# A state-space layer and a mixture of experts in one launch: the moments of z1 taken by squares on ACT, the projection put between the two shared down products, and the first tile table made from six groups

## The reference

```python
def reference(x, A, B, C, D, gamma, beta, router_weight, ...):   # x: 2 x 2048 x 256, float32
    xB = einsum('bsd,nd->bsn', x, B)
    state = tanh(state @ A.T + xB_t)              # a scan over the 2048 steps
    y = einsum('bsn,dn->bsd', states, C) + D * x + x
    x = layernorm(x + layernorm(y) * gamma + beta)          # x2
    # router: sigmoid, the better of 2 groups of 4 experts, the best 2 of its 4, weights divided by their sum
    routed = sum over the 2 chosen e of w_e * (silu(x @ w_gate[e]) * (x @ w_up[e])) @ w_down[e]
    shared = (silu(x @ sw_gate) * (x @ sw_up)) @ sw_down
    return layernorm(x + routed + shared)
```

## Time and profile before

| | |
|---|---|
| median of three runs | 330.69 us (330.62 to 330.85) |
| the profiled execution, its own time | 330.8 us |
| its span, first to last instruction | 329.1 us |
| scan, first pass, and loads | to about 44 us |
| seven periods | about 44 to 161 us; from p = 2 on one is 14.72 us |
| group 7 and first table | to 176.5 us |
| 43 tiles | 176.5 to about 315 us |
| busy, share of the span | PE 83%, DVE 70%, POOL 50%, ACT 47% |

### The profile page before, as it was taken

The page is one execution under the profiler, slowest core; times in us unless marked ns, Lnnn a source line. Parts: engine busy times, 40 slices in busy tenths (PEclk is TensorE's granted clock), DMA queues, the critical chain, the costliest instruction groups (busy, mean ns, idle before and its releaser), DMA issues.

```text
span 329.1 us, 7496 instructions
## 1 busy us (share of the span) xinstructions
PE 274.0 (83%) x2237; PEld 225.2 (68%) x2237; DVE 229.9 (70%) x912; ACT 154.9 (47%) x354; POOL 163.4 (50%) x302
## 2 busy tenths in 40 slices
PE   4998997788888989886476899999999999999920
PEld 4897986687777878775354567777777777677610
DVE  4366977769898989889893688866666656656630
ACT  1464522554445465453520445655655655654620
POOL 3102004037686776768643426545555555555571
PEclk9999999799999999999676699999999999999995
DMA  5898920001130303022136823545444353431100
GB/s 178 273 279 260 375 96 2 0 2 67 67 122 11 133 0 132 33 101 89 43 132 189 253 84 72 156 124 154 116 133 135 89 143 121 121 95 51 34 7 0
DMA packets 21002, 36.79 MB, mean 112 GB/s; under 512 B 3029, under 2 KB 9694, under 8 KB 20961
## 3 DMA queue, kind: packets, MB, share of 16 engines
q1 hardware_dynamic: 16336, 23.50, 24.9%
q0 software_dynamic: 4624, 12.79, 10.2%
HBM read 20.00 MB, written 17.71 MB: 115 GB/s over the span
## 4 chain that ended last, share of the span: by engine, by line
PE 65%; DVE 11%; SPq 6%; issue 6%; ACT 5%; POOL 3%; DMA 2%; POOLq 1%; DVEq 0%
PE bank L658 21%; PE bank L685 11%; PE bank L602 5%; PE bank L614 4%; PE bank L549 4%; PE bank L546 4%; PE bank L506 4%; SPq L410 4%; PE bank L626 3%; PE bank L673 3%; PE bank L513 2%; PE bank L561 2%; DMA rows<-in_L_attn_x_dram 2%; DVE st L992 2%; ACT xT L805 2%
## 5 line engine op out<-in xcount | busy, mean ns | idle before, releaser
L658 PE MATMUL bank<-w,xTt 128*128 x516 | 69.7, 280 | 7.9 <-ACT xTt L823 2.2
L658 PEld LDWEIGHTS bank<-w,xTt 128*128 128x128 f16 x516 | 45.4, 99 | 36.4 <-issue 30.3
L1429 POOL DMA_INDIRECT out_dram<-xT,where x43 | 44.6, 1037 | 36.1 <-ACT xT L841 28.8
L1195 DVE SCALAR_TENSOR_TENSOR th_<-bank,tw,tsg 128x128 f32<-128x128 f32 x86 | 26.2, 346 | 34.1 <-ACT tsg L829 32.5
L829 ACT ACTIVATE tsg<-bank,g_un 128x256 f32<-128x256 f32 x43 | 20.4, 474 | 60.4 <-PE bank L658 60.4
L685 PE MATMUL bank<-wd,thT 128*128 x172 | 46.6, 393 | 0.1
L1415 POOL DMA_INDIRECT xs_dram<-rows,slot_i x32 | 33.5, 1046 | 18.1 <-issue 10.7
L506 PE MATMUL bank<-xT,BT 128*128 128x128 f32 x256 | 41.0, 284 | 0.0
L1372 POOL TENSOR_TENSOR rstd<-mv,eps 128x2 f32<-128x2 f32 (+2 forms) x38 | 10.4, 275 | 53.3 <-DVE mv L1209 21.9
L506 PEld LDWEIGHTS bank<-xT,BT 128*128 128x128 f32 x256 | 35.0, 196 | 0.4
L1376 POOL TENSOR_TENSOR rstd<-rstd,neghalf 128x2 f32<-128x2 f32 (+2 forms) x38 | 32.2, 848 | 0.6
(11 more groups left out here) (188 smaller groups left out, 540.1 us busy)
## 6 DMA issues: line engine op xcount, KB each, us to landing
xT<-xs_dram SPq DMA_DIRECT2D x43, 262.0 KB, 3.0
rows<-in_L_attn_x_dram SPq DMA_DIRECT2D x7, 512.0 KB, 7.1
xs_dram<-cmp SPq DMA_DIRECT2D x1, 3144.0 KB, 14.5
wd<-in_L_ffn_w_down_dram SPq DMA_DIRECT2D x1, 1024.0 KB, 10.2
out_dram<-xT,where POOLq DMA_INDIRECT x43, 2.7
rows<-in_L_attn_x_dram SPq DMA_DIRECT2D x2, 256.0 KB, 3.6
xs_dram<-rows,slot_i POOLq DMA_INDIRECT x32, 3.0
xs_dram<-cmp SPq DMA_DIRECT2D x1, 262.0 KB, 15.8
```

What stands on the lines that cost most here:

```text
L658: last = pe.matmul(ps_tu(j)[:, r, :, :].rearrange("p w i -> p (w i)"), xTt[:, j % 2, 2 * px + k, :], w16[:, pw, bass.ds(e, 1), k, :, :].re ...
L1195: stt(th_[:, j % 2, r, :], ps_tu(j)[:, r, 1, :], tw[:, j % 4, r:r + 1], tsg[:, j % 2, r, :], ALU.mult, ALU.mult).then_inc(th_ready, 1)
L1429: nc.gpsimd.indirect_dma_start(out=out_rows, out_offset=bass.IndirectOffsetOnAxis(ap=where[:, j:j + 1], axis=0), in_=trow(j)[:, DM:2 * DM] ...
```

## The change

The moments of z1 are no longer statistics on DVE. `b` gives the row sums as an accumulator output (`accum_out`), a new token `c` on POOL turns them into minus the mean, `B` becomes four `Square` activations on ACT with that as the bias and the sum of squares as an accumulator output, and `R` starts from those sums and has three operations in place of four. In the period, A stands between the two W; the steps of the scan stand after the first U and after L, ahead of the second U; Z(n+1) moves into the next period, behind E; V is split in two and two, around c; R stands ahead of w. The first table takes in groups 0 to 5 and 13 tiles in place of groups 0 to 6 and 16, and its eight parts stand ahead of E of group 6.

```diff
-    CHECKS = ((G - 2, 16), (G - 1, 27))
+    CHECKS = ((G - 3, 13), (G - 1, 30))
...
-        put(("A", 0), ("M", 0), ("r", 0), ("S", 0), ("b", 0), ("B", 0), ("R", 0))
+        put(("A", 0), ("M", 0), ("r", 0), ("S", 0), ("b", 0), ("c", 0), ("B", 0), ("R", 0))
         scan(T4)
         put(("A", 1), ("X", 0, 0), ("X", 0, 1))
...
             if o >= 0:
-                put(("E", o), *[("V", o, t) for t in range(T4)])
-            put(("S", p), ("U", n), ("s", n), ("L", g), ("Q", g), ("U", n + 1), ("s", n + 1))
+                put(("E", o), ("Z", 2 * o + 1), ("V", o, 0), ("V", o, 1))
+            put(("S", p), ("U", n), ("s", n))
             if more:
                 scan()
-            put(("b", p), ("H", n), ("W", n), ("B", p), ("R", p), ("Z", n), ("H", n + 1))
+            put(("L", g), ("Q", g))
             if more:
                 scan()
-            put(("W", n + 1))
+            put(("b", p), ("c", p), ("H", n), ("U", n + 1), ("W", n))
+            if o >= 0:
+                put(("V", o, 2), ("V", o, 3))
+            put(("B", p), ("s", n + 1))
             if more:
                 put(("A", p + 1))
-            else:
-                put(("meet", 0))
-            put(("D", g), ("w", g), ("X", p, 0), ("X", p, 1), ("Z", n + 1))
+            put(("D", g), ("R", p), ("w", g), ("H", n + 1), ("W", n + 1), ("Z", n), ("X", p, 0), ("X", p, 1))
...
-        put(("E", g - 1), *[("V", g - 1, t) for t in range(T4)])
         put(("U", n), ("s", n), ("L", g), ("Q", g), ("U", n + 1), ("s", n + 1))
         put(*[("N", 0, part) for part in range(PARTS)])
+        put(("E", g - 1), ("Z", 2 * g - 1), *[("V", g - 1, t) for t in range(T4)])
...
+            def second_moments(g):
+                act.wait_ge(centre_ready, g + 1)
...
+                for t in range(T4):
+                    nc.scalar.activation(squares[:, t, :], y1[:, g % 2, t, :], ACT.Square, bias=rstd[:, 1, 2, t:t + 1],
+                                         accum_out=zsq[:, g % 2, t:t + 1]).then_inc(squared, 1)
...
+            def centre(g):
+                pool.wait_ge(z1_done, (g + 1) * T4)
...
+                nc.gpsimd.tensor_scalar(rstd[:, 1, 2, :], zsum[:, g % 2, :], -1.0 / DM, None, ALU.mult).then_inc(centre_ready, 1)
+            def second_rsqrt(g):
+                pool.wait_ge(squared, (g + 1) * T4)
```

More of the change, by code:

```diff
@@ L119, in period @@
             if o >= 0:
-                put(("E", o), *[("V", o, t) for t in range(T4)])
-            put(("S", p), ("U", n), ("s", n), ("L", g), ("Q", g), ("U", n + 1), ("s", n + 1))
+                put(("E", o), ("Z", 2 * o + 1), ("V", o, 0), ("V", o, 1))
+            put(("S", p), ("U", n), ("s", n))
             if more:
                 scan()
-            put(("b", p), ("H", n), ("W", n), ("B", p), ("R", p), ("Z", n), ("H", n + 1))
+            put(("L", g), ("Q", g))
             if more:
                 scan()
-            put(("W", n + 1))
+            put(("b", p), ("c", p), ("H", n), ("U", n + 1), ("W", n))
+            if o >= 0:
+                put(("V", o, 2), ("V", o, 3))
+            put(("B", p), ("s", n + 1))
             if more:
                 put(("A", p + 1))
-            else:
-                put(("meet", 0))
-            put(("D", g), ("w", g), ("X", p, 0), ("X", p, 1), ("Z", n + 1))
+            put(("D", g), ("R", p), ("w", g), ("H", n + 1), ("W", n + 1), ("Z", n), ("X", p, 0), ("X", p, 1))
         for p in range(1, G):
             period(p)
+        put(("meet", 0))
         assert not steps
@@ L241, in x2cols @@
             return x2T[:, :, g * GT:(g + 1) * GT].bitcast(F16).rearrange("p k (a t) -> p a k t", a=2)
-        st = sb("st", [P, 2, T4, 6])
-        mv = sb("mv", [P, 2, T4, 2])
+        st = sb("st", [P, 1, T4, 6])
+        mv = sb("mv", [P, 1, T4, 2])
         rstd = sb("rstd", [P, 2, 4, T4])
@@ L249, in ssm_moe_kernel @@
         neghalf = sb("neghalf", [P, T4])
+        zsum, zsq, squares = sb("zsum", [P, 2, T4]), sb("zsq", [P, 2, T4]), sb("squares", [P, T4, DM])
         eps = sb("eps", [P, T4])
@@ L801, in second @@
                 nc.scalar.activation(rows16[:, tiles_, 0, :], xskip[:, tiles_, :], ACT.Copy, scale=XS).then_inc(x2_high, 1)
+            def second_moments(g):
+                act.wait_ge(centre_ready, g + 1)
+                if g >= 2:
+                    act.wait_ge(rstd2_ready, g - 1)
+                if g:
+                    act.wait_ge(squared, g * T4)
+                for t in range(T4):
+                    nc.scalar.activation(squares[:, t, :], y1[:, g % 2, t, :], ACT.Square, bias=rstd[:, 1, 2, t:t + 1],
+                                         accum_out=zsq[:, g % 2, t:t + 1]).then_inc(squared, 1)
             def keep_x2(g, half):
@@ L847, in _ @@
                     step(L + n, states[:, n, :])
+                elif kind == "B":
+                    second_moments(n)
                 elif kind == "X":
@@ L1009, in normed @@
                     stt(y1[:, par, t, :], y1[:, par, t, :], rstd[:, 0, 1, t:t + 1], xres[:, g * T4 + t, :],
-                        ALU.mult, ALU.add).then_inc(z1_done, 1)
-            def second_moments(g):
-                par = g % 2
-                for t in range(T4):
-                    dve.wait_ge(z1_done, g * T4 + t + 1)
-                    nc.vector.bn_stats(st[:, 1, t, :], y1[:, par, t, :]).then_inc(st2_done, 1)
-                for t in range(T4):
-                    dve.wait_ge(st2_done, g * T4 + t + 1)
-                    nc.vector.bn_aggr(mv[:, 1, t, :], st[:, 1, t, :]).then_inc(mv2_done, 1)
+                        ALU.mult, ALU.add, accum_out=zsum[:, par, t:t + 1]).then_inc(z1_done, 1)
             def low(g, half):
@@ L1224, in _ @@
                     normed(n)
-                elif kind == "B":
-                    second_moments(n)
                 elif kind == "Y":
@@ L1406, in weigh @@
                 assert done == (g + 1) * WEIGH_STEPS, done
+            def centre(g):
+                pool.wait_ge(z1_done, (g + 1) * T4)
+                if g:
+                    pool.wait_ge(x2_ready, T4 * g)
+                nc.gpsimd.tensor_scalar(rstd[:, 1, 2, :], zsum[:, g % 2, :], -1.0 / DM, None, ALU.mult).then_inc(centre_ready, 1)
+            def second_rsqrt(g):
+                pool.wait_ge(squared, (g + 1) * T4)
+                nc.gpsimd.tensor_scalar(rstd[:, 1, 0, :], zsq[:, g % 2, :], 1.0 / DM, LN_EPS, ALU.mult, ALU.add).then_inc(second_step, 1)
+                pool.wait_ge(second_step, 2 * g + 1)
+                nc.gpsimd.tensor_tensor(rstd[:, 1, 1, :], rstd[:, 1, 0, :], neghalf[:, :], ALU.pow).then_inc(second_step, 1)
+                pool.wait_ge(second_step, 2 * g + 2)
+                nc.gpsimd.tensor_tensor(rstd[:, 1, 3, :], rstd[:, 1, 2, :], rstd[:, 1, 1, :], ALU.mult).then_inc(rstd2_ready, 1)
             def scatter(g, t):
@@ L1438, in _ @@
                 elif kind == "R":
-                    rsqrt(mv2_done, (n + 1) * T4, mv[:, 1, :, :], rstd[:, 1, :, :], rstd_step, steps, rstd2_ready)
-                    steps += 2
+                    second_rsqrt(n)
+                elif kind == "c":
+                    centre(n)
                 elif kind == "w":
```

2 lines of the change are left out of this document (1 added, 1 removed).

## The result

The changed kernel takes 346.62 us (median of 4 runs, 344.96 to 347.85) beside 330.77 for the kernel before (330.62 to 332.8): ratio of the runs 1.0429, 95% interval 1.038 to 1.0478 (the two medians alone give 1.048), 15.9 us slower. The sign of the forecast of 337.4 was right, and the size was not: the time lies above the range. The profiled execution of after has a span of 346.0 us, 16.9 more than the 329.1 of before. Executions of one kernel differ by up to 2%, so where the traced one is long, only the stages named are read from it.

The account below looks back on a forecast made before the run. PE and DVE, each busy 12.95 of 14.70 us a period, were taken as the bound. Opening less periods 2.7, group 7 3.3 and the end 0.7 make 6.7 us over 330.69: 337.4, range 331.5 to 341.5.

Parts of the forecast that it names:

- The step that failed: The 43 PE-bound tiles behind group 7: the same work before and after, only their start counts, so no time added.
- the four terms: Start to X(1) 8.2 us lost, six steps to X(7) 5.5 gained, then 3.3 lost to the tiles, 0.7 after them.
- The opening: Up to X(1): tanh 4 to 7 queue behind group 0's squares on ACT, PE idles, its clock falls; 8.2 us later.
- The read-outs: Reading out accumulators: 0.16 us each on ACT, 0.64 for four; 0.10 each on DVE, 0.40 for four in b.
- The periods: X(1) to X(7): a loop through POOL's queue sets 14.1 us a period; six steps 84.6 for 90.1, 5.5 us gained.
- Rival (3): The loop through POOL doesn't hold; periods fall to PE's 12.97 us, total 330.6, not slower; chance 0.14.
- The lowest sum: Lowest period of the loop through POOL, with no read-outs and all scatters at 0.97 us: 13.45 us.
- Group 7: X(7) to the first tile: L(7) waits for E(6) behind the first table, U at the lower clock; 3.3 us lost.
- The end: Last normalisation is the pair (41, 42), with two sends ahead of it on POOL; 0.7 us lost, between nothing and 2.4.
- Rival (2): PE's clock doesn't fall at the opening and group 7: less 1.7 and 1.4 us, total 334.3; chance 0.15.
- Rival (4): Square isn't in ACT's held function set: 16 loads of 1.28 us, 20 us, total 358; chance 0.03.
- Rival (5): Read-outs and DVE's loop share at their highest, clock low through all of A(1): 2.3 + 4.8, about 343; chance 0.06.

Follow-up runs that it names:

- tables of 12 and 31: Changed kernel with tables of 12 and 31 tiles, group 0's squares behind four tanh, most first-table parts behind E of group 6, no padding: 330.63 us, 0.9604.
- the mended loads with the opening alone: Changed kernel with register loads aligned to four words, and group 0's squares and R behind the tanh of steps 4 to 7: 329.66 us, 0.9954 of before.
- with group 7 alone: Changed kernel with register loads aligned to four words, and only the first of the first table's eight parts ahead of E(6): 331.65 us, 0.9988 of before.

## Why the prediction missed

**The step that failed** is "They are the same work before and after, so what counts is when the first of them starts". The products are the same. But the number 13 in `CHECKS` also sets where the second table begins in memory, and the register load is 0.67 us longer from there. In the sum the tiles stood as 0; they are 11.1 us. Without them the forecast of 6.7 stands against 5.8. I had priced the smaller first table (less work for the table, the last pair, the fetch that waits for less) and never the loads, which are 22 instructions of PE's queue that no busy share counts. Nothing in the trace of before shows a load from such a start; its row (328/333/569 ns) shows only that the loads are there. That 5.8 lies so near 6.7 is in part luck: the four terms were off by -0.9, -1.1, +0.5 and +0.6.

**The opening**: right in mechanism. M(1)'s second half came at 64.69, forecast 64.5, with some luck: the lower clock cost 2.2 us for the 1.7 charged (1.0 in the steps to the fourth tanh, 1.2 behind it), and the squares ended 0.3 sooner. X(1) followed in 11.02, forecast 12.1: B takes 2.08 and not 2.73, and the squares start 3.27 behind the first U (68.63 to 71.90), where I had 3.75.

**The read-outs** were mis-sized. On DVE I took 0.10 each: the trace shows four of 0.08, of which three lie under the next operation, so b goes from 51.58 to 53.29, 1.71 us for 1.67. The rule of the Trainium skill (VectorE: DVE Perf Modes, "Two Vector instructions with no wait between them"), that an accumulator output makes two instructions, agrees with these rows. On ACT I took 0.16 each; the row is 0.19 long, and the steps of 0.49 are no longer than the 0.50 that I had taken for an activation without it.

**The periods**: 13.85 for 14.1, with R released by the last scatter, as worked out. The difference is mostly the read-outs of b, which stand in the loop ahead of c. Rival (3), a period at PE's floor of 12.97, fell: PE is busy for 13.01 and waits for 0.84. The lowest sum, given as 13.45, left out that c waits for b; with that it is 13.7 by the same rows.

**Group 7**: 3.8 for 3.3, the wait, the lower clock and H(15)'s idle time of 3.07 as told, though PE idled 3.75 in front of L(7) and not 5.

**The end**: 1.3 for 0.7; tables of 12 and 31 brought this stretch back, as the mechanism has it, though not the time from the first tile on. Two sends of some 2.4 us ahead of the last normalisation cost more than half of themselves in this stretch.

**Rival (2)**, the clock that doesn't fall, fell with the 0.50 of 52 to 62 us. Rival (4) fell: one table load for the whole kernel (1.28 us), and squares of 0.49. Rival (5) fell, as its read-outs were to be longer, and they are shorter; its terms add up to 344.5 and not to 343, which is nearer to the time measured and for another reason. **The chances**: "slower" had 0.87, and the range was too narrow because it held only the bounds of what I had listed.

## What to carry to other kernels

A number in a plan can set addresses as well as work: after a change to a split or a count, list what is laid out by it, and compare the durations of the small queue instructions (register loads above all) by line, before and after, along with the busy shares. Here, keep blocks of four words that are loaded to registers at multiples of four words, or make the split point even. And where ACT's queue holds both a scan's next step and work that waits for a long chain, put the step first: 2 us of squares cost 4.7 here, through an idle PE and its clock.

## What the runs showed of the hardware

- PE's register load of four words took 0.33 us where it started at a multiple of four words, and 1.00 us where it started two words behind one, in both kernels (medians); no other start was tried. PE's products stood for about 0.8 us in each such place (12.6 us in 16 places, 16.5 in 21).
- Three chips ran the unchanged kernel before in 343 to 345 us and two earlier sets elsewhere in 331 to 332. Some 9 us of the difference are periods in which the logits' tanh on ACT starts 2 to 4 us late while POOL scatters; it is on time without scatters (step 14.72) or with the scatters behind it (15.24). Another 3.5 lie in the tiles. Whether chip or time decides, and why, stays open. By this the changed kernel stands at 1.043 on one chip and 1.013 on another. The mended kernel with tables of 12 and 31 stood at 0.96 on three chips; where before takes 331 to 332 it never ran, and there the mended loads with the opening alone stood at 0.995, and with group 7 alone at 0.999.
- PE's idle time of 6.6 us, to 55.94, was followed by scan steps and the first products of a projection at the lower clock (0.50 over 52 to 62 us), and 0.99 in the 2 us behind. In before an idle time of 2.84 us was followed by 0.53 over 3.6 us.
